# A graph layer on one core: the first of four blocks of edges put in order by POOL's scatters instead of by one-hot products

## The reference, cut to what matters

```python
xn = _layernorm(x)
x = x + gnn(xn, W_w, W_b, a_w, a_b, row=src, col=dst) + mix(xn, Wq, Wkv, Wproj, bproj)
x = x + moe(_layernorm(x), router_w, w1, b1, w2, b2)

# gnn: for every edge (row, col)
Wh = x @ W_w + W_b
e = leaky_relu((Wh @ a_w[:256])[col] + (Wh @ a_w[256:])[row] + a_b[0])
att = softmax of e over the edges with the same row
h = relu(segment_sum(att[:, None] * Wh[col], row))
```

## Time and profile before

| what | before |
|---|---|
| time, median of 3 runs | 2222.33 us (2213.17 to 2228.12) |
| span of the profiled execution, first to last instruction | 2207.5 us |
| busy: PE, DVE, ACT, POOL | 1718.1, 1669.8, 976.2, 994.8 us |
| chain that ended last | DVE 42%, PE 23%, issue 16%, unknown queue 10%, ACT 4% |
| POOL's first gather of table rows starts at | 511.11 us |

### The profile page before, as it was taken

The page is one execution under the profiler, slowest core; times in us unless marked ns, Lnnn a source line. Parts: engine busy times, 40 slices in busy tenths (PEclk is TensorE's granted clock), DMA queues, the critical chain, the costliest instruction groups (busy, mean ns, idle before and its releaser), DMA issues.

```text
span 2207.5 us, 40303 instructions
## 1 busy us (share of the span) xinstructions
PE 1718.1 (78%) x13588; PEld 1259.6 (57%) x13588; DVE 1669.8 (76%) x4220; ACT 976.2 (44%) x2300; POOL 994.8 (45%) x988
## 2 busy tenths in 40 slices
PE   3778785574785688888757888887888888889998
PEld 2557573463674466666535555555555555566666
DVE  5998998663566677776767887888888888886665
ACT  6322221121332233222235656666666656575655
POOL 3000003425566655655666666666666666640000
PEclk7898997796898788888968999999999999999999
DMA  5011111124554444333333333333333333860000
GB/s 174 16 59 52 51 66 32 42 84 115 145 165 130 118 120 119 102 94 90 90 90 87 86 90 83 94 83 94 82 95 92 86 92 83 89 56 11 11 20 13
DMA packets 121460, 182.21 MB, mean 83 GB/s; under 512 B 21490, under 2 KB 91902, under 8 KB 121214
## 3 DMA queue, kind: packets, MB, share of 16 engines
q0 software_dynamic: 45312, 120.06, 23.3%
q1 hardware_dynamic: 75904, 59.25, 8.6%
HBM read 152.43 MB, written 26.63 MB: 81 GB/s over the span
## 4 chain that ended last, share of the span: by engine, by line
DVE 42%; PE 23%; issue 16%; another core or an unknown queue 10%; ACT 4%; DVEq 2%; POOL 1%; DMA 0%; SPq 0%; ACTq 0%; POOLq 0%
PE bank L1255 6%; PE bank L1271 5%; DVE mloc L1615 4%; DVE big L1518 4%; DVE scr L1637 3%; DVE big L1523 3%; DVE work L1809 3%; DVE big L1520 2%; DVE big L1525 2%; DVE big L1796 2%; DVE scr L1483 2%; DVE work L1593 2%; DVE work L1610 2%; PE bank L947 1%
## 5 line engine op out<-in xcount | busy, mean ns | idle before, releaser
L664 POOL DMA_INDIRECT work<-table,tiles x904 | 921.0, 1019 | 546.6 <-PE bank L1142 277.8
L1271 PE MATMUL bank<-big 128*128 128x256 f16 x2352 | 327.7, 278 | 34.8 <-issue 34.5
L1255 PE MATMUL bank<-scr,big 128*128 128x512 f16 (+1 forms) x1248 | 282.3, 377 | 0.3 <-ACT big L871 0.3
L1140 PE MATMUL bank<-work,scr 128*128 128x257 f16 x904 | 269.9, 299 | 13.0 <-issue 10.5
L1271 PEld LDWEIGHTS bank<-big 128*128 128x128 f16 x2352 | 232.3, 99 | 78.3 <-issue 46.0
L1141 PE MATMUL bank<-work,scr 128*128 128x256 f16 x904 | 270.8, 300 | 5.9 <-issue 5.6
L1142 PE MATMUL bank<-work,scr 128*128 128x257 f16 x904 | 268.9, 297 | 5.9 <-issue 5.9
L1637 DVE SCALAR_TENSOR_TENSOR scr<-scr,gg,bank 128x257 f32<-128x257 f32 x452 | 216.7, 479 | 29.7 <-remote 16.6
L999 PE MATMUL bank<-big 128*128 128x208 f16 x1568 | 176.9, 269 | 67.7 <-DVE big L1525 60.9
L799 ACT ACTIVATE work<-bank 128x1024 f16<-128x1024 f16 x113 | 115.5, 1022 | 242.7 <-DVE mloc L1615 144.0
L999 PEld LDWEIGHTS bank<-big 128*128 128x128 f16 x1568 | 150.7, 102 | 94.6 <-issue 88.9
(11 more groups left out here) (340 smaller groups left out, 3494.1 us busy)
## 6 DMA issues: line engine op xcount, KB each, us to landing
work<-table,tiles POOLq DMA_INDIRECT x904
scr<-normed_cols SPq DMA_DIRECT2D x98, 128.0 KB
table<-big SPq DMA_DIRECT2D x49, 129.0 KB, 2.1
normed_rows<-scr SPq DMA_DIRECT2D x49, 128.5 KB, 2.6
big<-normed_rows SPq DMA_DIRECT2D x49, 128.5 KB
normed_cols<-big SPq DMA_DIRECT2D x49, 128.0 KB, 1.7
xs<-in_x_dram SPq DMA_DIRECT2D x4, 1536.0 KB, 14.2
out_dram<-work SPq DMA_DIRECT2D x48, 128.0 KB
```

The costliest lines, as they stand in the source:

```text
L664: pool.indirect_dma_start(G[:, r, j, :], None, table, bass.IndirectOffsetOnAxis(ap=col[:, t:t + 1], axis=0)).then_inc(rows_in[r // GS], 16)
L1140: pe.matmul(of[:, 0:D + 1], hi, Gh[:, r, j, 0:D + 1], start=(j == 0), stop=False)
L1255: mm = pe.matmul(bank[5 + f][:, 0:n * P], w1p[pw][:, e, h, f * P:(f + 1) * P], x2p[b % 2][px][:, h, 0:n * P], start=(h + m == 0), stop=(h ...
L1271: mm = pe.matmul(of, hTp[ph][:, k % 2, f, (j + c) * P:(j + c + 1) * P], w2p[pw][:, e, f, :], start=False, stop=(f == 1 and m == 2))
```

## The change

Block 0 no longer goes through step 4. DVE packs its two values per edge into `recs0` and works out one index per edge (`ind0`). POOL then scatters the records of 4 bytes singly to a new DRAM tensor `sorted0`, one indirect transfer per column (128 records each, 200 transfers), waits for them all, and reads the ordered block back into `recs[:, 0]`. `sorted0` is zeroed by SP beforehand. POOL's copies of `vrow` for blocks 1, 2 and 3 now stand in the run of scatters, ahead of column 8, 64 and 136. The other three blocks are ordered as before, in 73 batches. `one_hots` of block 2 is written as one piece ahead of the ranks of block 1. `NODE_AT` now runs from batch 5 to batch 60 of 73.

```diff
-    BATCH = [0]
-    for a, z in COLS:
+    BATCH = [0, 0]
+    for a, z in COLS[1:]:
         BATCH.append(BATCH[-1] + (z - a) // NC)
...
-        NB0 = 10
-        NODE_AT = {NB0 + w * (BATCH[-1] - 1 - NB0) // (W - 1): w for w in range(W)}
+        NB0 = 5
+        NODE_AT = {NB0 + w * (BATCH[-1] - 13 - NB0) // (W - 1): w for w in range(W)}
+        FIRST_COLUMNS = COLS[0][1]
+        ROWS_AFTER = (0, 8, 64, 136)
...
# SP
+            sp.dma_start(sorted0.rearrange("(p t) c -> p (t c)", p=P), tiles[:, 0:TT].bitcast(F16)).then_inc(blank, 16)
...
-            sp.wait_ge(scattered, 16 * NBL * QT)
+            sp.wait_ge(scattered, 16 * (FIRST_COLUMNS + 1 + NBL * QT))
...
# POOL
+            rank_rows(0)
+            pool.wait_ge(blank, 32)
+            pool.wait_ge(s_ind, 1)
+            for c in range(FIRST_COLUMNS):
+                if c in ROWS_AFTER[1:]:
+                    rank_rows(ROWS_AFTER.index(c))
+                pool.indirect_dma_start(sorted0, bass.IndirectOffsetOnAxis(ap=ind0[:, c:c + 1], axis=0),
+                                        recs0[:, c, :], None).then_inc(scattered, 16)
+            pool.wait_ge(scattered, 16 * FIRST_COLUMNS)
+            pool.dma_start(recs[:, 0, :, :].rearrange("p t c -> p (t c)"),
+                           sorted0.rearrange("(p t) c -> p (t c)", p=P)).then_inc(scattered, 16)
...
# ACT: block 0 has no batches and no copy of the banks
-            for b in range(NBL):
+            for b in range(1, NBL):
...
# PE
+            column_ranks(0)
+            column_sums(1)
+            column_bases(1)
+            for b in range(1, NBL):
...
# DVE
+                if b == 0:
+                    for k, of in enumerate((v1h, v2h)):
+                        dve.tensor_copy(recs0[:, :, k], of[:, a:z])
+                    link(dve.tensor_scalar(si[:, 0:m], si[:, 0:m], (P * CH).bit_length() - 1, None, ALU.arith_shift_right))
+                    link(dve.scalar_tensor_tensor(srank[:, 0:m], si[:, 0:m], float(CH), bi[:, 0:m], ALU.mult, ALU.add))
+                    dve.scalar_tensor_tensor(ind0, ai[:, 0:m], float(TT), srank[:, 0:m], ALU.mult, ALU.add).then_inc(s_ind, 1)
+                    one_hots(2)
+                    column_counts(1)
+                    bases(1)
+                    continue
```

More of the change, by code:

```diff
@@ L53, in graph_layer @@
     COLS = [(a, min(a + BC, ECP)) for a in range(0, ECP, BC)]
-    BATCH = [0]
-    for a, z in COLS:
+    assert EREST >= COLS[0][1]
+    BATCH = [0, 0]
+    for a, z in COLS[1:]:
         BATCH.append(BATCH[-1] + (z - a) // NC)
@@ L79, in graph_layer @@
     normed_cols = nc.dram_tensor("normed_cols", [W * P, D], F32).ap()
+    sorted0 = nc.dram_tensor("sorted0", [P * TT, 2], F16).ap()
     binned = nc.dram_tensor("binned", [DUMP + NBL * QT * P, 2 * CH], F16).ap()
@@ L282, in graph_layer @@
         node = piece(T, dt=I32)
+        ind0 = piece(COLS[0][1], dt=I32)
+        recs0 = piece(COLS[0][1], 2, dt=F16)
         startw, stw, inw = (tiles[0:64, T + T // 2 + TT + n * NG:T + T // 2 + TT + (n + 1) * NG] for n in range(3))
@@ L358, in graph_layer @@
         (s_hot, s_col, s_colsb, s_base, s_v, s_rank, s_max, s_b, s_a, s_a1, s_a2, s_perm, s_rec, s_dest,
-         s_turned, s_list) = (sem("s_" + k) for k in (
+         s_turned, s_ind) = (sem("s_" + k) for k in (
              "hot", "col", "colsb", "base", "v", "rank", "max", "b", "a", "a1", "a2", "perm", "rec", "dest",
-             "turned", "list"))
+             "turned", "ind"))
         s_row = [sem(f"s_row{i}") for i in range(2)]
@@ L395, in graph_layer @@
         assert NG <= 512
-        NB0 = 10
-        NODE_AT = {NB0 + w * (BATCH[-1] - 1 - NB0) // (W - 1): w for w in range(W)}
+        NB0 = 5
+        NODE_AT = {NB0 + w * (BATCH[-1] - 13 - NB0) // (W - 1): w for w in range(W)}
         assert len(NODE_AT) == W and max(NODE_AT) < BATCH[-1]
         BASES_AT = 4
-        assert BATCH[1] > NB0 > BASES_AT
+        FIRST_COLUMNS = COLS[0][1]
+        ROWS_AFTER = (0, 8, 64, 136)
         VT = bank[0][:, :].bitcast(F16)
@@ L634, in _, with rank_rows @@
                       allow_small_or_imprecise_dtypes=True).then_inc(consts, 1)
-            for b, (a, z) in enumerate(COLS):
+            def rank_rows(b):
+                a, z = COLS[b]
                 n = (z - a) // 2
@@ L645, in _ @@
                                    of[:, 0:2 * n]).then_inc(s_row[b % 2], 16)
-            pool.wait_ge(blank, 16)
+            rank_rows(0)
[9 more added lines that the diff above has]
+                           sorted0.rearrange("(p t) c -> p (t c)", p=P)).then_inc(scattered, 16)
             for b in range(NBL):
                 pool.wait_ge(s_dest, b + 1)
-                pool.wait_ge(s_rec, b + 1)
+                if b:
+                    pool.wait_ge(s_rec, b)
+                else:
+                    pool.wait_ge(scattered, 16 * (FIRST_COLUMNS + 1))
                 for q in range(QT):
@@ L988, in permuted @@
             def permuted(b):
-                if b:
-                    pe.wait_ge(s_rec, b)
+                if b > 1:
+                    pe.wait_ge(s_rec, b - 1)
                 for n in range(BATCH[b], BATCH[b + 1]):
@@ L1072, in key_sums @@
                 mm.then_inc(k_sum, 1)
-            pe.wait_ge(s_rec, NBL)
+            pe.wait_ge(s_rec, NBL - 1)
             pe.wait_ge(tiles_in, 1)
@@ L1485, in _ @@
                     last.then_inc(s_max, 1)
-                    if b + 1 < NBL:
+                    if b != 1 and b + 1 < NBL:
                         one_hots(b + 1, k_ * W // len(chunks_b), (k_ + 1) * W // len(chunks_b))
+                    elif b == 1:
+                        pass
                     elif k_ == 0:
@@ L1506, in _ @@
                 for n in range(BATCH[b], BATCH[b + 1]):
-                    c, at = n * NC, (n - BATCH[b]) * NC
+                    c, at = a + (n - BATCH[b]) * NC, (n - BATCH[b]) * NC
                     if b + 1 < NBL and n == BATCH[b] + BASES_AT:
```

## The result

The changed kernel takes 2366.92 us in the median of 4 runs (2357.99 to 2376.32), the kernel before 2223.3 (2213.17 to 2228.12): a ratio of 1.0671 [1.0634, 1.0707], 144 us slower. The forecast was 2271, its range ended at 2330.

What follows compares the result with a forecast made beforehand. DVE was taken to bound the ordering, with everything behind starting from its end. Terms -65.8 (block 0), +10 (node work), -2 (last batch) and +107 (scatter delay) gave +49 us on 2222: 2271 us, range 2160 to 2330.

Steps and rivals of the forecast that it cites:

- +107, what the scatters do to TensorE's results: Ordering: 200 indirect scatters delay TensorE's results as DVE sees them, at 0.53 us each, adding 107 us.
- no-delay rival: Ordering: the dead stretches are not made by the scatters, so the change gains 58 us, 2164; chance 0.27.
- the top end of 150: Ordering: highest price of the scatter delay, 158 scatters beside batches at 0.95 us each, 150 us.
- dense rival: Ordering: each scatter beside a batch costs 0.95 us or more, POOL's run ends behind the batches; 2330, chance 0.11.
- TensorE's results are seen late: Ordering: while POOL issues indirect transfers without pause, DVE sees TensorE's results late; 39 scatters cost DVE 20.8 us.
- -65.8 for block 0: Start of ordering: 35.4 us stand in place of 101.2 before block 1's first batch, saving 65.8 us.
- +10 for denser node work: Batches with moved node windows: TensorE becomes slightly slower than DVE, adding 10 us.
- POOL adds nothing: Ordering: POOL's 200 scatters, read-back and old 39 scatters end before block 3's batches, adding 0 us.
- POOL is 24 us early: End of ordering: POOL's old 39 scatters end by 392 us, block 3's batches near 416.
- the trace shows no lengthening: POOL's issues beside DVE's one-hots: the trace shows no lengthening from a shared memory port.
- Slower: Whole kernel: the changed kernel is slower by more than about 1% (22 us); chance 0.54.

Runs made afterwards that it cites:

- e1: The changed kernel with its 200 scatters of block 0 left out, and what waits for them; slow session: 2143.53 us, 0.9675 of the kernel before.
- e9: The changed kernel itself, unaltered, timed again in a quick session: 1959.34 us, 0.9761 of the kernel before.
- e12: The kernel before, with POOL waiting for the landing of every third of its 39 scatters; quick session: 2009.22 us, 1.0008 of the kernel before.
- e16: The kernel before, with POOL waiting for the landing of every third of its 39 scatters; slow session: 2209.87 us, 0.9878 of the kernel before.
- e5: The changed kernel with 16 instead of 128 records in each of the 200 scatters; quick session: 1945.19 us, 0.9691 of the kernel before.
- e11: The changed kernel with 16 instead of 128 records in each of the 200 scatters, timed in another quick session: 1953.46 us, 0.9731 of the kernel before.
- e15: The changed kernel with POOL waiting for landing after every 4 of the 200 scatters; slow session: 2246.08 us, 1.0031 of the kernel before.
- e10: The changed kernel with POOL waiting for landing after every 4 of the 200 scatters; quick session: 2044.46 us, 1.0176 of the kernel before.
- e2: The changed kernel with 64 instead of 128 records in each of the 200 scatters; slow session: 2364.53 us, 1.0645 of the kernel before.
- e3: The changed kernel with 200 plain POOL transfers of the same records, stored unsorted, replacing the indirect ones; slow session: 2139.7 us, 0.9657 of the kernel before.
- e7: The changed kernel with POOL waiting for the landing of each of the 200 scatters; quick session: 2232.24 us, 1.1121 of the kernel before.

## Why the prediction was wrong

**The step that failed is "+107, what the scatters do to TensorE's results".** It measured +223 (2366.92 less e1's 2143.53), and +221 by the ratios. The mechanism was named rightly (indirect transfers of POOL hold up TensorE), and what was wrong is its size. Three things stand behind that.

First, the shape. I multiplied a price per scatter, 0.53 us, from the run of 39. The delay grows along an unbroken run, from next to nothing in its first 4 to 25 us to batches 35 to 59 us apart in place of 2.87, until 7 to 14 us after the start of its last scatter. The run of 39 cost 20.8 us. The runs of 56 (with eight more just ahead of it), 72 and 64, 71, 93 and 84 us long, cost 56, 84 and 70 us, summed from what DVE's batches took above their usual pitch: 1.1 us for each scatter. The rows had this: two and a half batches at full pace beside scatters, which the prediction noted, but under the no-delay rival. A price that grows along a run of 39 can't be multiplied up to runs of 72; the top end of 150 was 0.95 for 158 scatters, and even 200 of 0.95 would have been 190. The dense rival's clause, that POOL's row ends later still because it waits for bases, came true twice (31.56 and 89.13 us) and kept POOL's row from hiding under the ranks.

Second, "TensorE's results are seen late" was right, and only half of it. The matmuls themselves start up to 2.8 us apart as well, and the lateness was read as too small: by the rule of two batches, what DVE got at 419.54 in the kernel before were not the matmuls issued at 412.53 but the second half of the 32 from 394.14 to 397.55, 22 us old.

Third, what no row of one trace could show: the delay is there in some sessions and not in others. In quick ones the "no delay" rival (2164, or -58) is the right one: -48.

**The other terms.** -65.8 for block 0: e1 has the first batch of block 1 at 97.02 against the forecast 100.8, so -69.6; some three of the four microseconds are the ranks, which take less without one-hots between them. With the scatters in place (e9) it stands at 101.94, for a reason that wasn't foreseen: the first of POOL's 200 scatters takes 5.96 us and not 1.3, so `vrow` goes out at 81.90 (76.79 in e1). **+10 for denser node work: nothing**; e1 and e9 hold 2.87 us through nearly all batches with windows, and DVE waited for TensorE in front of them only 5.2 and 4.5 us up to 345 us. Together e1's last batch is 71.2 us earlier than before (399.95 against 471.14), and its time 73.4. **POOL adds nothing: wrong in the quick session.** e9's last batch is 62.7 us before e12's, its first gather 38.9. POOL's scatters start 1.40 us apart there and not 1.34, the read-back is issued at 357 and not before 340, and the 52 binned scatters follow to 433, 47 us behind the last batch. "POOL is 24 us early" set the end of the 39 at 392 and that of the batches at 416; in e9 the 39 end at 414 and the batches at 390, so POOL is 24 us late. The 416 carried the 20.8 us of dead time of the old kernel along. Of the 24 us the rest of the program gives some 9 back (the first gather is 39 earlier, the end 48); where those come from was not looked into. The prediction also says that "the trace shows no lengthening" of POOL's issues beside DVE's batches, and its own row has 1.14 us beside them and 0.97 behind the earlier trace rows; in the quick session this is the 1.40 us.

**Chances.** Slower had 0.54, and the sign was right for the session in which it was measured; 2366.92 lay outside 2160 to 2330 through the size of one term.

**What stays open.** What it is in POOL's indirect issues that makes TensorE's matmuls start late and its signals arrive late, which of the two comes first, and what makes a session slow. Every time on record is of an execution for which the profile's records (span and clock) exist as well, so whether the recording has a part in it isn't shown. The records give the same chip number for sessions 3 (quick) and 4 (slow); whether that was one chip at two times or two chips of that number isn't recorded, so it is not shown to belong to a chip. The 209 us between the kernels before (2217 and 2008) lie in the stretch of the 904 gathers, which are indirect transfers too: e16 (slow) and e12 (quick) are one kernel, their first gathers start at 492.0 and 486.0 us, their last at 1961.6 and 1753.6, and behind that they take 243 and 250 us. In between POOL waits 289 us for TensorE (line 1144) in the one and 74 in the other. That this is the same delay fits, and was not tested. No version tried is the best in both kinds of session: e16 is best in the slow (2209.87), the changed kernel in the quick (1959.34), e5 and e11 leave records out.

## What to carry to other kernels

Read a price per transfer from a trace only with its run: look where in the row of transfers the first wait stands and where the last, and extend the row, not the mean. A long unbroken row of indirect transfers on GpSimd beside a busy TensorE can bring both TensorE and those who wait for it almost to a stop; a short wait after every three or four of them cures it where it occurs and costs POOL's time everywhere. With POOL's time to spare that was a gain of 28 us (e16). With POOL nearly the bound it took 137 us of loss away in the slow session (e15) and left no gain, and cost 85 us in the quick one (e10 against e9). When an engine waits long, look up which instruction it waits for and when that one ran: it may have ended long ago. Before a gain or a loss is believed, time the unchanged kernel in the same session and look for "unknown" in its chain: here one and the same change is +6.7% or -2.4%.

## What the runs showed that I had not expected

- An indirect scatter of POOL takes 0.98 us with 0.30 us between two, with 128 records of 4 bytes as with 128 of 64 (0.97 at the end of the earlier trace rows), and 0.89 with 64 records (e2); the first of the 200 takes 5.96 us; a plain transfer of the same 128 records takes POOL 0.54 us and disturbs nobody (e3).
- In a slow session TensorE's short matmuls start 0.7, 1.4, 2.1 or 2.8 us apart beside an unbroken row of them, with the DMA engines at 2% and the granted clock at 0.51, and DVE sees TensorE's signals up to 55 us late.
- Beside DVE's batches an indirect issue of POOL lengthens from 0.97 us to between 1.02 and 1.57, in either kind of session.
- The kernel before itself takes 2008 us in a quick session and 2202 to 2245 in a slow one, nearly as much as the dearest change made here moved it (e7, +224).
